# Two routed layers on one core: the selector matmuls give way to an addition on GpSimd and to rows below the tables

## The chip, the cores and the metric

One core of one Trainium2 chip. The time is the device time of one launch in microseconds, median of several runs.

## The reference, cut to what matters

`x` is 128 sequences of 64 tokens of 256 features. Every sequence `b` has an expert `e0 = itok_B_0_7[b]` (of 8) and a domain `d = itok_B_0_15[b]` (of 16).

```
h = gelu(x @ Wi[e0] + bi[e0]);  o = h @ Wo[e0] + bo[e0]          # 256 -> 1024 -> 256
r = layernorm(o + x);           x1 = r * gamma[e0] + beta[e0]
a = gelu(x1 @ down_W.T + down_b)                                 # 256 -> 64
e = a @ expert_W[d].T + expert_b[d] + domain_emb[d]
out = layernorm(e @ up_W.T + up_b + x1) * ln_gamma + ln_beta
```

## The kernel before

Two sequences make a tile of 128 tokens; a sort on the chip puts sequences of one expert together, so that 60 tiles have one expert and the last four ("mixed") may have one for each half. The loop over tiles is a pipeline of 64 + 5 steps, written out by hand for each engine: in step `i` TensorE does the first product of tile `i`, the second of `i-1`, the transposes of `i-2`, the down product of `i-3` and the up product of `i-4`. Steps 6 to 53 run in a hardware loop of 8 steps a round, the others are unrolled. Engines wait for each other by counting semaphores; SyncE issues nearly all DMAs on one queue.

Every value that goes through TensorE is split into an f16 high part and an f16 low part, and a product is three matmuls (high x high, low x high, high x low), L1138 to L1140 and L1149 to L1151. Weights of an expert come in chunks of 128x512 (`stage`); ScalarE makes the high part (L619), VectorE the low one (L867). In the same way `x_T` (x with the features on the partitions) gives `x_hi` (L664) and `x_lo` (L863), gelu's result `h` (L695) gives `h_hi` (L706) and `h_lo` (L896), in two halves a tile.

The first residual `r` (L912) is taken from the PSUM bank `p_o` and `x_nat`, its statistics by L915 and L927, the power -1/2 of the variance on GpSimd (L584), the normal form `z` on VectorE (L950). TensorE turns it into `p_t` (L1187), ScalarE and VectorE scale it by gamma into `yT_hi` (L743) and `yT_lo` (L980), and the down product (L1162 to L1164) makes `p_d`. Gelu of it is `a` (L720), which is put into `a1s` as high part on all partitions (L725) and then as low part on the lower 64 (L938). `up` multiplies `a1s` with two tables of each sequence's domain (`ctab`, high and low part; expert_W and up_W are multiplied into one beforehand, entry by entry, in `rounds`), L1179, four matmuls. The second norm goes L922, L932, L943, power L588 on GpSimd, `y` L958; GpSimd multiplies by ln_gamma and adds ln_beta (L560, L562), and multiplies `z` by gamma for the second residual (L579, `yg`).

What depends on the expert or domain only as one row of 256 is added by a matmul with a selector: `sel_tile` (128x128, a 1 or a scale at the rows of this tile's sequences; copied by GpSimd from `sel`, L603) times `bo_parts` into `p_o` (L1256), the output bias, and times `parts` into `p_u` (L1175), everything that is added in the up product. Both have three f16 parts of each row. They are made at the start on GpSimd by `split_rows` (L524 to L528), `parts` in its step 1.

```
mm(p_u[:, 0:D], sel_tile[:, four, :], parts[:, :], start=True, stop=False)
...
mm(p_o[:, 0:D], sel_tile[:, (four + 3) % 4, :], bo_parts[:, :], start=True, stop=False)
```

## Time and profile before

| | before |
|---|---|
| median of 3 runs | 472.51 us (472.42 to 473.59) |
| the profiled execution's own time | 472.13 us |
| its span in the trace | 470.4 us |
| TensorE, VectorE, ScalarE, GpSimd busy | 448.5, 379.4, 350.8, 339.4 us |
| granted clock, mean | 0.988 |
| DMA moved | 44.38 MB, 94 GB/s |

PE is TensorE's matmuls, PEld its weight loads, DVE VectorE, ACT ScalarE, POOL GpSimd, SP SyncE; SPq and ACTq are their DMA issues. A row of the timeline has start and duration in us, engine, line, operation, output and inputs, and in square brackets how long the engine sat idle before it and whom it waited for. The start of a matmul's row is when it enters the array; its duration includes the pipeline, so the cost of a matmul is the distance to the next one.

### The profile page before, as it was taken

The page shows a single profiled execution, that of the slowest core. Times are in us where ns is not written, and L with a number is a line of the kernel's source. Part 1 is how long each engine was busy: PE and PEld are TensorE (multiplying, and loading weights), DVE is VectorE, ACT ScalarE, POOL GpSimd, SP SyncE. Part 2 cuts the span into 40 slices and gives each one's busy share as a digit, 9 for nine tenths or more (in the row PEclk, how much of TensorE's full clock was granted, in tenths as well). Part 3 has the DMA queues.
Part 4 walks back from the last instruction along what each step waited for, and adds up shares of the span by engine and source line. Part 5 has one row for each costly group of instructions (what it writes and reads, how often), then busy time and mean ns, then how long its engine had stood idle before and what let it go on. Part 6 is the DMA issues. An engine that isn't in the chain of part 4 may idle for free.

```text
span 470.4 us, 19196 instructions
## 1 busy us (share of the span) xinstructions
PE 448.5 (95%) x5856; PEld 414.9 (88%) x5857; DVE 379.4 (81%) x1052; ACT 350.8 (75%) x1094; POOL 339.4 (72%) x559
## 2 busy tenths in 40 slices
PE   3898999999999999999999999999999999999973
PEld 2687999999999999999999999999999999998961
DVE  7769888888888888888888888888888887776465
ACT  2689877787777877778777787777877767776721
POOL 5244777877778877897778977888788887764533
PEclk9999999999999999999999999999999999999995
DMA  4852244433433333334333343334432222221101
GB/s 104 289 166 80 68 107 122 113 93 102 106 104 103 92 104 106 106 97 110 92 102 99 103 106 90 104 96 106 106 92 81 57 63 66 64 58 36 26 24 33
DMA packets 66810, 44.38 MB, mean 94 GB/s; under 512 B 41537, under 2 KB 58322, under 8 KB 66642
## 3 DMA queue, kind: packets, MB, share of 16 engines
q1 hardware_dynamic: 65744, 43.68, 34.7%
q8 instruction: 21, 0.34, 0.3%
q10 hardware_dynamic: 1026, 0.21, 0.2%
q14 instruction: 19, 0.16, 0.1%
HBM read 35.47 MB, written 8.39 MB: 93 GB/s over the span
## 4 chain that ended last, share of the span: by engine, by line
PE 88%; DVE 4%; issue 2%; ACT 2%; POOL 1%; DMA 1%; POOLq 0%; ACTq 0%; DVEq 0%
PE p_o L1150 12%; PE p_o L1149 12%; PE p_o L1151 12%; PE p_h L1138 12%; PE p_h L1139 12%; PE p_h L1140 12%; PE p_u L1179 6%; PE p_t L1187 3%; PE p_u L1175 2%; PE p_d L1162 2%; PE p_o L1256 1%; PE p_d L1164 1%; PE p_d L1163 1%; ACT W L619 1%; DMA x_T<-in_xT 1%
## 5 line engine op out<-in xcount | busy, mean ns | idle before, releaser
L1138 PE MATMUL p_h<-x_hi,W 128*128 128x128 f16 (+1 forms) x1088 | 184.5, 217 | 1.0 <-DVE x_lo L863 0.5
L1139 PE MATMUL p_h<-x_lo,W 128*128 128x128 f16 (+1 forms) x1088 | 184.4, 217 | 0.0
L1140 PE MATMUL p_h<-x_hi,W 128*128 128x128 f16 (+1 forms) x1088 | 184.3, 217 | 0.0
L695 ACT ACTIVATE h<-p_h,bi_tile 128x128 f32<-128x128 f32 (+1 forms) x544 | 148.6, 358 | 0.0
L1151 PE MATMUL p_o<-W,h_lo 128*128 x512 | 139.6, 273 | 0.0
L1150 PE MATMUL p_o<-W,h_hi 128*128 x512 | 139.6, 273 | 0.0
L1149 PE MATMUL p_o<-W,h_hi 128*128 x512 | 139.6, 273 | 0.0
L1138 PEld LDWEIGHTS p_h<-x_hi,W 128*128 x1088 | 105.9, 98 | 5.4 <-issue 2.8
L1139 PEld LDWEIGHTS p_h<-x_lo,W 128*128 x1088 | 106.0, 98 | 1.3
L1140 PEld LDWEIGHTS p_h<-x_hi,W 128*128 x1088 | 106.0, 98 | 0.0
L588 POOL TENSOR_TENSOR rs<-mv,neg_half 128x1 f32<-128x1 f32 x64 | 55.5, 866 | 60.0 <-DVE mv L943 60.0
L720 ACT ACTIVATE a<-p_d,gb_tile 128x128 f32<-128x128 f32 (+1 forms) x68 | 24.1, 360 | 87.2 <-PE p_d L1164 87.2
L896 DVE SCALAR_TENSOR_TENSOR h_lo<-h,h_hi 128x512 f16<-128x512 f32 (+1 forms) x128 | 83.9, 658 | 1.6 <-ACT h_hi L706 1.6
L706 ACT ACTIVATE h_hi<-h 128x512 f16<-128x512 f32 (+1 forms) x128 | 79.1, 621 | 2.0
L603 POOL COPY sel_tile<-sel 128x128 f16 (+1 forms) x64 | 77.7, 1213 | 0.6 <-issue 0.6
L938 DVE SCALAR_TENSOR_TENSOR a1s<-a,a1s 64x128 f16<-64x128 f32 x64 | 18.5, 290 | 49.5 <-ACT a1s L725 49.3
L560 POOL TENSOR_TENSOR y<-y,lng 128x256 f32<-128x256 f32 x60 | 43.6, 726 | 19.2 <-DVE h_lo L896 17.0
L1150 PEld LDWEIGHTS p_o<-W,h_hi 128*128 128x128 f16 x512 | 50.1, 98 | 5.8
L1151 PEld LDWEIGHTS p_o<-W,h_lo 128*128 128x128 f16 x512 | 50.1, 98 | 5.8
L1149 PEld LDWEIGHTS p_o<-W,h_hi 128*128 128x128 f16 x512 | 50.1, 98 | 4.4
L584 POOL TENSOR_TENSOR rs<-mv,neg_half 128x1 f32<-128x1 f32 x64 | 35.4, 553 | 24.3 <-DVE mv L927 24.3
L980 DVE SCALAR_TENSOR_TENSOR yT_lo<-p_t,gb_tile,yT_hi 128x128 f16<-128x128 f32 (+1 forms) x136 | 39.5, 333 | 12.2 <-ACT yT_hi L743 12.2
(179 smaller groups left out, 899.8 us busy)
## 6 DMA issues: line engine op xcount, KB each, us to landing
stage<-in_w SPq DMA_DIRECT2D x56, 256.0 KB, 2.7
x_nat<-in_x SPq DMA_DIRECT2D x128, 64.0 KB, 2.1
out<-y SPq DMA_DIRECT2D x128, 64.0 KB, 2.0
x_T<-in_xT SPq DMA_DIRECT2D x126, 64.0 KB, 2.2
W<-in_w SPq DMA_DIRECT2D x8, 256.0 KB, 3.6
g_t<-in_gamma SPq DMA_DIRECT2D x1, 1024.0 KB, 8.0
W<-in_expert_W SPq DMA_DIRECT2D x2, 128.0 KB, 3.0
upT<-in_up_W SPq DMA_DIRECT2D x2, 64.0 KB, 2.6
```

The costliest lines, as they stand in the source:

```text
L560: pool.tensor_tensor(last, last, lng[:, :], ALU.mult).then_inc(zg_done, 1)
L588: pool.tensor_tensor(rs[:, 1:2], mv[:, 1, 1:2], neg_half[:, 0:1], ALU.pow).then_inc(rs2_done, 1)
L603: pool.tensor_copy(sel_tile[:, four, :].rearrange("p (n s) -> p n s", n=2), sel[:, bass.ds(2 * i, 2)].unsqueeze(2).to_broadcast([P, 2, S]))\
L695: ins = nc.scalar.activation(h[:, c, mine], p_h[parity][:, c, mine], ACT.Gelu, bias=bi_tile[:, parity, n, c:c + 1], scale=1.0 / (XS * WS))
L706: ins = nc.scalar.activation(out, h[:, cols_h, mine], ACT.Copy, scale=HS)
L896: ins = v.scalar_tensor_tensor(lo[at], h[:, cols_h, mine], HS, hi[at], ALU.mult, ALU.subtract)
L1138: mm(out, hi, x_hi[:, parity, k, mine], start=(k == 0), stop=False)
L1139: mm(out, hi, x_lo[:, parity, k, mine], start=False, stop=False)
L1140: ins = mm(out, lo, x_hi[:, parity, k, mine], start=False, stop=(k == KD - 1))
L1149: mm(p_o[:, 0:D], h_high[at], hi, start=False, stop=False)
L1150: mm(p_o[:, 0:D], h_high[at], lo, start=False, stop=False)
L1151: ins = mm(p_o[:, 0:D], h_low[at], hi, start=False, stop=(j == KI - 1 and n == len(places) - 1))
```

## The change

1. The output bias is added on GpSimd: `bo_t` holds `bo` of all experts on all partitions (one more broadcast load of 1,024 KB, issued ahead of `g_t`), and in step `i` GpSimd adds tile `i-1`'s row to `x_nat` between the two powers. The first residual waits for that (`xb_done`) and not for the load.
2. What is added in the up product lies in `ctab` itself. The low part of the table has only 64 rows; rows 64 to 90 of it now hold the added rows in three f16 parts (3 of the entry itself, 24 of the experts). `parts` goes out to a DRAM tensor after step 1 of SyncE and comes back into these rows with four DMAs in step 2. A second block `a1o` (91 rows used) has the high part of `a` above and constants below: ScalarE writes it after `yT_hi`, with a scale and a bias for each partition (`keeps`, and a fourth column of `gb_tile`). `up` is `a1s` x high, `a1o` x low and added rows, for each of the two sequences.
3. `sel`, `sel_tile`, its copy on GpSimd, both selector matmuls and what made them at the start (on VectorE, TensorE, GpSimd and ScalarE) are gone.
4. `x_T`, `x_hi`, `x_lo` are laid out as (sequence, feature half, 64 tokens): a load of a sequence is 512 B a partition in one piece, and the moving operand of the first product has two runs of 64 columns.
5. SyncE reads the record of two steps at once; VectorE does `y` (`normal_2`) behind the weight chunk and not ahead of it.

```diff
+        bo_t = sb("bo_t", [P, E0 * D])
-        x_hi = sb("x_hi", [P, 2, KD, P], f16)
+        x_hi = sb("x_hi", [P, 2, 2, KD, S], f16)
...
@@ SyncE
+            sp.dma_start(bo_t[:, :], t["bo"].partition_broadcast(P)).then_inc(bo_in, 16)
             sp.dma_start(g_t[:, :], t["gamma"].partition_broadcast(P)).then_inc(g_in, 16)
...
+                    if parity == 0:
+                        two = 12 if exists(i + 1 + 2) or exists(i + 1 - 5) else 6
+                        record[:] = indices(sp, 6 * i + IDX_SP, two, B - 1)
...
+                if isinstance(i, int) and i == 1:
+                    sp.wait_ge(parts_ready, 1)
+                    sp.dma_start(added[:, :], parts[0:PARTS * GROUP, :]).then_inc(added_out, 16)
+                if isinstance(i, int) and i == 2:
+                    sp.wait_ge(added_out, 16)
+                    by_part = added[:, :].rearrange("(q g) c -> q g c", g=GROUP)
+                    sp.dma_start(ctab[OWN_ROWS, :, 1, :], by_part[:, 0:ENTRIES, :]).then_inc(added_in, 16)
+                    for q in range(PARTS):
+                        sp.dma_start(ctab[A + PARTS + E0 * q:A + PARTS + E0 * (q + 1), :, 1, :],
+                                     by_part[q, ENTRIES:ENTRIES + E0, :].unsqueeze(1)
+                                     .to_broadcast([E0, ENTRIES, D])).then_inc(added_in, 16)
@@ GpSimd
-            pool.wait_ge(b_ready, 1)
-            split_rows(b_s[:, :], b_rest, b_16, bo_parts)
...
                     pool.tensor_tensor(rs[:, 0:1], mv[:, 0, 1:2], neg_half[:, 0:1], ALU.pow).then_inc(rs1_done, 1)
+                if exists(i - 1):
+                    pool.wait_ge(xnat_in[1 - parity], loads(i - 1, 1 - parity, 2))
+                    if isinstance(i, int) and i == 1:
+                        pool.wait_ge(bo_in, 16)
...
+                        pool.tensor_tensor(x_nat[:, 1 - parity, :], x_nat[:, 1 - parity, :],
+                                           bo_t[:, bass.ds(e_last * D, D)], ALU.add).then_inc(xb_done, 1)
...
-                    need(pool, a1_done, i - 3)
+                    need(pool, a1o_done, i - 3)
...
-                    pool.tensor_copy(sel_tile[:, four, :].rearrange("p (n s) -> p n s", n=2),
-                                     sel[:, bass.ds(2 * i, 2)].unsqueeze(2).to_broadcast([P, 2, S]))\
-                        .then_inc(sel_done, 1)
@@ ScalarE, behind yT_hi
+                if exists(i - 3):
+                    for n in range(2 if mixed(i - 3) else 1):
+                        mine = slice(n, n + 1) if mixed(i - 3) else slice(0, 2)
+                        ins = nc.scalar.activation(own(a1o[:, :, :])[:, mine, :],
+                                                   a1[:, :].rearrange("p (n s) -> p n s", n=2)[:, mine, :],
+                                                   ACT.Identity, scale=keeps[:, :],
+                                                   bias=gb_tile[:, 1 - parity, n, KD + 1:GB])
+                    ins.then_inc(a1o_done, 1)
@@ VectorE
-                    dve.wait_ge(xnat_in[parity], loads(i - 2, parity, 2))
+                    dve.wait_ge(xb_done, i - 1)
...
-                if exists(i - 4):
-                    normal_2()
                 for j, (m, place_n, slot_n) in chunks(i, weights):
                     dve.wait_ge(w_hi, j + 1)
                     low(m, place_n, stage[:, slot_n, :]).then_inc(w_lo, 1)
+                if exists(i - 4):
+                    normal_2()
@@ TensorE
-                    pe.wait_ge(sel_done, i - 3)
-                    mm(p_u[:, 0:D], sel_tile[:, four, :], parts[:, :], start=True, stop=False)
                     pe.wait_ge(a1_lo, i - 3)
+                    pe.wait_ge(a1o_done, i - 3)
                     for n in range(2):
-                        for part in range(2):
-                            ins = mm(p_u[:, 0:D], a1s[:, n, :], up_weights(n, part), start=False,
-                                     stop=(n == 1 and part == 1))
+                        mm(p_u[:, 0:D], a1s[:, n, :], up_weights(n, 0), start=(n == 0), stop=False)
+                        ins = mm(p_u[:, 0:D], a1o[LOW_ROWS, n, :], up_weights(n, 1), start=False, stop=(n == 1))
...
-                    pe.wait_ge(sel_done, i)
-                    mm(p_o[:, 0:D], sel_tile[:, (four + 3) % 4, :], bo_parts[:, :], start=True, stop=False)
```

GpSimd's queue in one step of the hardware loop, before: the two products of the output (`y`), `yg`, the two powers, then the copies for gamma and for the selector.

```order
L560 TENSOR_TENSOR y<-y,lng 128x256 [waits hlo_half]
L562 TENSOR_TENSOR y<-y,lnb 128x256 [waits zg_done]
L579 ISA [waits z1_done]
L579 TENSOR_TENSOR yg<-z,g_t 128x256
L584 TENSOR_TENSOR rs<-mv,neg_half 128x1 [waits mv1_done]
L588 TENSOR_TENSOR rs<-mv,neg_half 128x1 [waits mv2_done]
L596 ISA [waits a1_done]
L596 COPY gb_tile<-gb_c 128x3
```

The same step in the changed kernel:

```order
L590 TENSOR_TENSOR y<-y,lng 128x256 [waits hlo_half]
L592 TENSOR_TENSOR y<-y,lnb 128x256 [waits zg_done]
L609 ISA [waits z1_done]
L609 TENSOR_TENSOR yg<-z,g_t 128x256
L614 TENSOR_TENSOR rs<-mv,neg_half 128x1 [waits mv1_done]
L618 ISA
L630 ISA [waits xnat_in0]
L630 TENSOR_TENSOR x_nat<-x_nat,bo_t 128x256
L635 TENSOR_TENSOR rs<-mv,neg_half 128x1 [waits mv2_done]
L643 ISA [waits a1o_done]
L643 COPY gb_tile<-gb_c 128x4
```

The addition stands between the two powers, and gamma's copy waits for `a1o`.

TensorE's up product in the hardware loop, before:

```order
L1175 MATMUL p_u<-parts,sel_tile 128x256 [waits sel_done,r2_done]
L1179 MATMUL p_u<-ctab,a1s 128x256 [waits a1_lo]
L1179 MATMUL p_u<-ctab,a1s 128x256 x3
```

and in the changed kernel:

```order
L1207 MATMUL p_u<-ctab,a1s 128x256 [waits a1o_done,a1_lo,r2_done]
L1208 MATMUL p_u<-ctab,a1o 128x256
L1207 MATMUL p_u<-ctab,a1s 128x256
L1208 MATMUL p_u<-ctab,a1o 128x256
```

One matmul is gone, and the whole group waits for `a1o` ahead of its first.

## Rows read from the trace of the kernel before

**Rows 1.** Window (length; PE, PEld, DVE, ACT, POOL busy; clock, DMA); chain by engine.

```profile
110.00:360.00 250.00, 249.96 (x3288) 235.57 (x3287) 210.56 (x574) 200.14 (x615) 201.02 (x307) 1.00 0.38 101
...
PE 88%; DVE 4%; issue 2%; ACT 2%; POOL 1%; DMA 1%; POOLq 0%; ACTq 0%; DVEq 0%
```

**Rows 2.** Chain in order (start, us, what); timeline of one step (start, us, engine, line, operation).

```profile
236.41 0.44 PE p_u L1179 x4
...
242.92 0.44 PE p_u L1179 x4
...
242.65 0.27 PE L1175 MATMUL p_u<-parts,sel_tile 128*128 128x256 f16 x1
...
245.88 0.27 PE L1256 MATMUL p_o<-bo_parts,sel_tile 128*128 128x256 f16 x1
```

**Rows 3.** ScalarE in the same step, and the group of `a1s` by line.

```profile
241.72 0.64 ACT L706 ACTIVATE h_hi<-h 128x512 f16<-128x512 f32 x1
...
244.40 0.37 ACT L720 ACTIVATE a<-p_d,gb_tile 128x128 f32<-128x128 f32 x1 [1.23 <-PE p_d L1164]
...
L725 ACT ACTIVATE a1s<-a 128x128 f16<-128x128 f32 x64 | 19.9, 311 | 2.0
```

**Rows 4.** The same step on VectorE, then GpSimd, then TensorE's transposes.

```profile
239.70 0.41 DVE L950 TENSOR_SCALAR z<-r,mv,rs 128x256 f32<-128x256 f32 x1
...
241.29 0.68 DVE L896 SCALAR_TENSOR_TENSOR h_lo<-h,h_hi 128x512 f16<-128x512 f32 x1
...
245.21 0.29 DVE L938 SCALAR_TENSOR_TENSOR a1s<-a,a1s 64x128 f16<-64x128 f32 x1 [0.79 <-ACT a1s L725]
...
245.65 0.65 DVE L896 SCALAR_TENSOR_TENSOR h_lo<-h,h_hi 128x512 f16<-128x512 f32 x1
...
242.21 0.72 POOL L560 TENSOR_TENSOR y<-y,lng 128x256 f32<-128x256 f32 x1
...
244.39 0.55 POOL L584 TENSOR_TENSOR rs<-mv,neg_half 128x1 f32<-128x1 f32 x1
245.81 0.89 POOL L588 TENSOR_TENSOR rs<-mv,neg_half 128x1 f32<-128x1 f32 x1 [0.88 <-DVE mv L943]
...
240.79 0.38 PE L1187 MATMUL p_t<-ident,z 128*128 128x128 f32 x2
```

**Rows 5.** Timeline at 43 us: GpSimd and VectorE at once.

```profile
43.11 0.73 POOL L579 TENSOR_TENSOR yg<-z,g_t 128x256 f32<-128x256 f32 x1
...
43.18 1.22 DVE L867 SCALAR_TENSOR_TENSOR W<-stage,W 128x512 f16<-128x512 f32 x1
```

**Rows 6.** Timeline of TensorE in a mixed tile: columns of 128, then of 64.

```profile
431.00 0.22 PE L1162 MATMUL p_d<-yT_hi,down_hi 128*128 128x128 f16 x1
...
431.17 0.19 PE L1138 MATMUL p_h<-x_hi,W 128*128 128x64 f16 x1
...
431.52 0.20 PE L1138 MATMUL p_h<-x_hi,W 128*128 128x64 f16 x1
```

**Rows 7.** Start: SyncE's issue, ScalarE's wait, and the window with its DMA share.

```profile
18.91 0.42 SPq L429 DMA_DIRECT2D g_t<-in_gamma  x1
...
28.03 0.42 ACT L664 ACTIVATE x_hi<-x_T 128x256 f16<-128x256 f32 x1 [1.32 <-DMA x_T<-in_xT]
...
22.00:26.00 4.00, 4.00 (x60) 3.52 (x58) 2.62 (x6) 3.97 (x12) 0.54 (x3) 1.00 1.02 370
```

**Rows 8.** Start: GpSimd's first split and first power, TensorE's first down.

```profile
25.52 0.40 POOL L524 CAST W<-W 128x256 f16<-128x256 f32 x1
...
35.05 0.90 POOL L584 TENSOR_TENSOR rs<-mv,neg_half 128x1 f32<-128x1 f32 x1 [4.58 <-DVE mv L927]
...
40.30 0.23 PE L1162 MATMUL p_d<-yT_hi,down_hi 128*128 128x128 f16 x1 [1.03 <-DVE yT_lo L980]
```

**Rows 9.** Drain: ScalarE's last `yT_hi` and TensorE's up group.

```profile
459.84 0.93 ACT L743 ACTIVATE yT_hi<-p_t,gb_tile 128x64 f16<-128x64 f32 x4 [1.75 <-POOL gb_tile L596]
...
460.47 0.37 PE L1175 MATMUL p_u<-parts,sel_tile 128*128 128x256 f16 x1 [0.74 <-issue]
```

More of the change, by code:

```diff
@@ L88, in build @@
         ident = sb("ident", [P, P])
-        sel = sb("sel", [P, SLOTS], f16)
-        parts = sb("parts", [P, D], f16)
-        bo_parts = sb("bo_parts", [P, D], f16)
+        keeps = sb("keeps", [P, 1])
         x_nat = sb("x_nat", [P, 2, D])
-        x_T = sb("x_T", [P, 2, KD, P])
-        x_hi = sb("x_hi", [P, 2, KD, P], f16)
-        x_lo = sb("x_lo", [P, 2, KD, P], f16)
+        x_T = sb("x_T", [P, 2, 2, KD, S])
+        x_hi = sb("x_hi", [P, 2, 2, KD, S], f16)
+        x_lo = sb("x_lo", [P, 2, 2, KD, S], f16)
         r1 = sb("r1", [P, D])
@@ L114, in build @@
         a1s = sb("a1s", [P, 2, P], f16)
-        a1_own = a1s[:, :, :].rearrange("p n t -> p (n t)")
+        a1o = sb("a1o", [P, 2, P], f16)
         st2 = sb("st2", [P, 9])
@@ L506, in _ @@
             link(pool.memset(embb[HALF[0], :, :], 0.0))
-            link(pool.memset(parts[:, :], 0.0))
-            link(pool.memset(bo_parts[:, :], 0.0))
+            link(pool.memset(keeps[:, :], 0.0))
+            link(pool.memset(keeps[HALF[0], :], AS))
+            takes = gb_c[:, :, KD + 1]
+            link(pool.memset(takes, 0.0))
+            link(pool.memset(gb_c[OWN_ROWS, :, KD + 1], AS * CS))
+            for q in range(PARTS):
+                link(pool.affine_select(out=takes, in_=takes, compare_op=ALU.not_equal, fill=AS * CS,
+                                        base=-(A + PARTS + E0 * q), pattern=[[-1, E0]], channel_multiplier=1))
             pool.wait_ge(emb_in, 2 * 16)
@@ L663, in high_x @@
                 need(act, s1_half, 2 * i - 2)
-                nc.scalar.activation(x_hi[:, parity, :, :], x_T[:, parity, :, :], ACT.Copy, scale=XS)\
+                nc.scalar.activation(flat(x_hi, parity), flat(x_T, parity), ACT.Copy, scale=XS)\
                     .then_inc(xhi_done, 1)
@@ L724, in step @@
                     need(act, up_done, i - 3)
-                    nc.scalar.activation(own(P), a1[:, :].rearrange("p (n s) -> p n s", n=2), ACT.Copy, scale=AS)\
+                    nc.scalar.activation(own(a1s[:, :, :]), a1[:, :].rearrange("p (n s) -> p n s", n=2), ACT.Copy, scale=AS)\
                         .then_inc(a1_hi, 1)
@@ L1137, in first_product @@
                         out = p_h[parity][:, c, mine]
-                        mm(out, hi, x_hi[:, parity, k, mine], start=(k == 0), stop=False)
-                        mm(out, hi, x_lo[:, parity, k, mine], start=False, stop=False)
-                        ins = mm(out, lo, x_hi[:, parity, k, mine], start=False, stop=(k == KD - 1))
+                        x_high, x_low = [x[:, parity, n:n + 1, k, :] if mixed(i) else x[:, parity, :, k, :]
+                                         for x in (x_hi, x_lo)]
+                        mm(out, hi, x_high, start=(k == 0), stop=False)
+                        mm(out, hi, x_low, start=False, stop=False)
+                        ins = mm(out, lo, x_high, start=False, stop=(k == KD - 1))
                 return ins
```

117 lines of the change are left out of this document (53 added, 64 removed).

## The prediction

> **What bounds the kernel now.** I read the windows first, since a mean over the span mixes stages. From 110 to 360 us TensorE is busy 249.96 of 250 us, VectorE 210.56, ScalarE 200.14, GpSimd 201.02 [rows 1], and the chain of waits that ended last is 88% TensorE [rows 1]. The chain's rows for the four up matmuls stand 6.51 us apart [rows 2]: the step of one tile is TensorE's own queue, full, at the full clock (1.00 in the window). A matmul taken out of it is worth its pitch, as long as nobody else needs more than the shorter step. So three questions remain: what the others have in hand in a step, and what the change does to start and drain, where TensorE does wait.
>
> **Selector matmuls, -13.5 us.** A step loses the `sel_tile` x `parts` matmul at the head of `up` (at 242.65) and the `sel_tile` x `bo_parts` one at the head of the second product (at 245.88) [rows 2]. Four matmuls of the same 256 columns take 0.44 us in the chain [rows 2], 0.11 each; the duration 0.27 in a row is pipelined and is not the price. The up itself keeps four. 64 tiles give 128 matmuls; two before 40 us and three in the drain stand where TensorE waits anyway, so 123 x 0.11 = 13.5 us. The step becomes 6.51 - 0.22 = 6.29 us.
>
> **ScalarE's block, 0.** `a1o` is one more 128x128 activation, as `a1s`, 0.31 us [rows 3]. ScalarE idles 1.23 us a step before `a` [rows 3]; 1.23 - 0.22 - 0.31 leaves 0.70. Its place is between `yT_hi` and `h_hi`, so it starts where `h_hi` does now, 241.72, and ends at 242.03; TensorE comes to `up` at 242.65 [rows 2, 3], now 0.11 earlier. Margin 0.5 us. Behind it are `h_hi`, `x_hi` and the next weight chunk, each 0.31 later; what VectorE makes of that `h_hi` starts only at 245.65 [rows 4]. Were the idle time gone, the cost would be 0.1 us a step or more.
>
> **GpSimd and VectorE, +1.0 us.** GpSimd loses the copy of the selector and gains `x_nat + bo`, a 128x256 tensor_tensor like `y * lng`, 0.72 us [rows 4]. It isn't the length that matters but the place. Now GpSimd starts `y` once VectorE's `h_lo` is through (241.29 + 0.68 = 241.97) and works to the end of the first power at 244.39 + 0.55 = 244.94, 2.73 us after its start, in the stretch in which VectorE reads PSUM or takes statistics. Then it pauses 0.88 us [rows 4], and the new addition falls into that pause: about 244.7 to 245.5. VectorE wants `a1s` at 245.21, an instruction with two SBUF inputs. What such a meeting costs shows at 43 us: GpSimd's `yg` ran from 43.11 to 43.84, and VectorE's `W`, sent at 43.18, took 1.22 us, where `h_lo` of the same 128x512 takes 0.68 [rows 4, 5]: it stood until 0.12 us before GpSimd's end. As a loop: from `a1s` to the end of the next `h_lo` VectorE needs 241.97 + 6.51 - 245.21 = 3.27 us without a gap; from there to the end of GpSimd's addition are 2.73 + 0.72 = 3.45. If `a1s` waits it out each time, the loop is 3.27 + 3.45 - 0.12 = 6.60 us. If `a1s` comes ahead of the addition, the next `h_lo`, 0.44 us behind it, waits in its place, and the loop is 6.60 - 0.44 = 6.16. A step of 6.29 lies between them, so I expect the two to alternate with VectorE up to 0.45 us late. That is bearable: `z` ends at 240.11 and TensorE turns it at 240.79 [rows 4], 0.68 ahead, 0.57 after the change. I charge 0.02 us for each of some 47 full steps, 1.0 us; the ends are 0 and 47 x 0.31 = 14.6 us. Moving `y` behind the weight chunk gives the second power, now behind the addition, 0.6 us more time, and costs nothing.
>
> **Moving operand in two runs, 0.** `x_hi` and `x_lo` are now two runs of 64 columns in a 128-column matmul. No row has this form. The last tiles show 64-column matmuls, twelve in 431.52 - 431.17 = 0.35 us, 0.029 each, and 128-column ones, three in 0.17, 0.056 each [rows 6]. As two separate matmuls each would cost 0.058: 48 a step make at most 0.1 us, some 6 us in all. The low end is 0, and I take it, since the columns are the same in number; a gain is excluded.
>
> **Start, +3.0 us.** SyncE puts `bo` for all experts (1,024 KB, as `g_t`) ahead of `g_t` at 18.9 us. The queue is full then: 1.02 of the DMA engines' time and 370 GB/s from 22 to 26 us, and ScalarE waited 1.32 us for `x_T` of tile 2, which stood behind `g_t` [rows 7]. 1.05 MB more at 370 GB/s is 2.8 us. ScalarE takes this wait ahead of tile 1's gelu, tables and `h_hi`, so all of it moves by 2.8, and so do VectorE's first residual and `z`, and the `yT_lo` for which TensorE waited 1.03 us at 40.30 [rows 8]. GpSimd is delayed as well: it now waits for `x_nat` of tile 0 (in the queue behind `x_T`, so not before 30.8), adds, and only then splits the rows, 25.52 to 35.05 - 4.58 = 30.47 now, until some 36.6; it has 4.58 us to spare before the power at 35.05 [rows 8], which will be wanted at 37.9. It has to read its indices first, so I add 0.2. Ends: 0, if the shorter list of packets for `x_T` (512 B and not 256 B) and the earlier tile rows pay it back, and 5, if GpSimd is late by 2 us more. SyncE's new wait for `parts_ready`, to some 36.6, holds back `x_T` of tile 4, two natural tiles and a chunk; none is wanted before the first down, at 40.30 now and 43.3 then. The transfers of the added rows go out in step 2 and are read by `up` of step 4, a step of 6.5 us behind that down: 0. Two steps' records in one load save SyncE some register loads; nobody waits for those.
>
> **Drain, +1.0 us.** There ScalarE's order is `yT_hi` of the last tile, then `a1o` of the one before, in two halves. `yT_hi` runs from 459.84 to 460.77, and TensorE began the up group at 460.47 [rows 9]; now that must wait for `a1o`, at about 461.2: later by 0.4 net. The last up waits for one more block behind `a1s`, 0.2. At step 64 `h_hi` is 0.4 later and the first residual with it, for which TensorE stood ready.
>
> **The sum**, against the profiled execution's own 472.1 us (span 470.4): 472.1 - 13.5 + 1.0 + 3.0 + 1.0 = 463.6. The median of the runs lies 0.4 higher, at 472.5, so 464.0 us, or 1.8% less. Measurement can tell about 0.3% (1.4 us) from no change.
>
> **The rivals.**
> - *The start does not get longer* (chance 0.15). For: TensorE at 30.9 us does not itself wait for tile 2 now, and packets of `x_T` are halved. Against: ScalarE's visible wait. 464.0 - 3.0 = 461.0, and 460 if VectorE's lateness is free too.
> - *GpSimd's addition sets the step: slower* (0.11). If `a1s` loses the race each time, the loop of 6.60 us is longer than the 6.51 of before, whatever TensorE saved. For: the addition starts 2.73 us after `h_lo`, and VectorE would be there after 6.29 - 3.27 = 3.02, so at first it does lose. Against: once it is late, it meets the addition in the other order. It decides from the point where VectorE can't be 0.3 us late without TensorE waiting for `z`. Price 47 x 0.31 = 14.6 instead of 1.0: 477.6 us. The Trainium skill, SBUF — State Buffer, "Who interferes with whom", has the rule: a VectorE instruction with two SBUF inputs and a GpSimd one that reads SBUF exclude each other, and the second to issue waits for the whole of the first. The meeting at 43 us agrees, up to the last 0.12 us.
> - *In between* (0.14): half of the steps lose, or two runs cost 0.1 us a step: 468 to 472.
> - *It doesn't do what it says* (0.02): TensorE finds a new wait at `up` on `a1o` each step; 472 or a little more.
> The forecast itself has 0.58, with 461.5 to 468.
>
> Faster by over 0.3% than 472.5 are the forecast, the first rival and nearly all between: 0.85; within 0.3% 0.04; slower 0.11. The range, with the lower rival in and the slow one out, is 459.0 to 471.0.
>
> **What would show it.** Right: up groups 6.29 us apart in the chain, TensorE still full from 110 to 360, `a1s` or the `h_lo` behind it lengthened by 0.2 to 0.5 us under GpSimd's addition; ScalarE's idle time before `a` near 0.7 us; its wait for `x_T` of tile 2 near 4 us, and TensorE at its first down at about 43.3. Wrong: up groups at 6.5 us or more, TensorE idle before the transposes on `z` (then it is the port) or before `up` (then `a1o`); 128-column matmuls on `x_hi` over 0.056 apart.

## The result, and the profile after

| | before | changed |
|---|---|---|
| median | 472.47 us (471.86 to 473.59, 4 runs) | 468.88 us (468.71 to 469.13, 4 runs) |
| span of the profiled execution | 470.4 us | 467.0 us |
| TensorE, VectorE, ScalarE, GpSimd busy | 448.5, 379.4, 350.8, 339.4 us | 435.8, 392.2, 378.4, 343.1 us |
| first up product | 46.77 | 50.28 us |
| from there to the up of tile 54 | 352.44 | 344.52 us |
| from there to the end | 71.19 | 72.20 us |

The ratio is 0.9923, with a 95% interval of 0.9909 to 0.9937: 3.6 us faster, where 8.5 were forecast. The last three rows of the table cut the span into start, 54 steps, and end, by the times at which an up group begins. The sum of the three changes is +3.5 - 7.9 + 1.0 = -3.4 us. The forecast was near for the start (+3.0); the steady part should have given 10.9, and the end should have got 0.65 shorter, where it got 1.0 longer.

The window of 250 us of the changed kernel (columns as in [rows 1]) and its matmuls at a round of the hardware loop, which begins every eighth step:

```profile
110.00:360.00 250.00, 248.59 (x3296) 231.89 (x3294) 223.47 (x588) 221.11 (x668) 205.08 (x314) 1.00 0.36 102
```

```profile
210.00 0.27 PE L1207 MATMUL p_u<-ctab,a1s 128*128 x1
...
216.42 0.23 PE L1168 MATMUL p_h<-x_hi,W 128*128 128x128 f16 x1 [0.29 <-issue]
...
216.91 0.27 PE L1207 MATMUL p_u<-ctab,a1s 128*128 x1
```

TensorE was busy all the time before [rows 1]; now 1.4 us are missing from the window. VectorE has 12.9 us more to do in it, though the change gave it nothing new there. The ordinary step is 6.30 us, as forecast (6.29). The step in which the loop turns round is 6.91 (210.00 to 216.91); before it was 6.71 (209.90 to 216.61), so it did not lose 0.22 but gained 0.20. The first matmul of the new round starts 6.42 us after the up group, where in an ordinary step it starts at 5.96.

An ordinary step on VectorE and GpSimd, the one that answers to [rows 4], and ScalarE's to [rows 3]:

```profile
241.26 0.68 DVE L933 SCALAR_TENSOR_TENSOR h_lo<-h,h_hi 128x512 f16<-128x512 f32 x1
...
244.64 0.29 DVE L974 SCALAR_TENSOR_TENSOR a1s<-a,a1s 64x128 f16<-64x128 f32 x1 [0.47 <-ACT a1s L759]
245.07 0.99 DVE L933 SCALAR_TENSOR_TENSOR h_lo<-h,h_hi 128x512 f16<-128x512 f32 x1
245.99 0.40 DVE L986 TENSOR_SCALAR z<-r,mv,rs 128x256 f32<-128x256 f32 x1
...
242.02 0.73 POOL L590 TENSOR_TENSOR y<-y,lng 128x256 f32<-128x256 f32 x1 [0.95 <-DVE h_lo L933]
...
244.71 0.81 POOL L630 TENSOR_TENSOR x_nat<-x_nat,bo_t 128x256 f32<-128x256 f32 x1
...
241.36 0.52 ACT L785 ACTIVATE a1o<-a,gb_tile,keeps 128x128 f16<-128x128 f32 x1
243.82 0.37 ACT L754 ACTIVATE a<-p_d,gb_tile 128x128 f32<-128x128 f32 x1 [0.60 <-PE p_d L1194]
```

GpSimd's addition (244.71 to 245.52) starts while `a1s` runs and is over 0.45 us after `h_lo` was sent; that `h_lo` takes 0.99 instead of 0.65, so it stood about 0.34, until 0.1 us before the addition's end. `z` ends at 246.39, 4.21 us after the up group of its step (242.18), not 3.97, and VectorE's `h_lo` of the first half 5.40 after it and not 5.15. This is the second of the two forecast orders (`a1s` first, `h_lo` held up). The forecast had the two alternate; here it is the second in nearly all steps. `a1o` takes 0.52 us, not 0.31. It ends 6.02 us after the up group, and TensorE's next up stands at 6.30.

The start, to be held against [rows 7, 8], and TensorE's waits in the last steps, of which before there were none for ScalarE's block:

```profile
29.99 0.42 ACT L698 ACTIVATE x_hi<-x_T 128x256 f16<-128x256 f32 x1 [4.58 <-DMA x_T<-in_xT]
...
30.56 0.88 POOL L630 TENSOR_TENSOR x_nat<-x_nat,bo_t 128x256 f32<-128x256 f32 x1 [15.34 <-DMA x_nat<-in_x]
...
38.42 0.56 POOL L614 TENSOR_TENSOR rs<-mv,neg_half 128x1 f32<-128x1 f32 x1 [1.81 <-issue]
...
415.65 0.27 PE L1207 MATMUL p_u<-ctab,a1s 128*128 x1 [0.90 <-ACT a1o L785]
...
452.06 0.27 PE L1207 MATMUL p_u<-ctab,a1s 128*128 x1 [1.76 <-ACT a1o L785]
...
457.10 0.37 PE L1207 MATMUL p_u<-ctab,a1s 128*128 x1 [2.08 <-ACT a1o L785]
...
460.45 0.37 PE L1207 MATMUL p_u<-ctab,a1s 128*128 x1 [1.70 <-ACT a1o L785]
```

### The profile page after: what moved, and what is told of

The parts are those of the page before. It is cut to its first block, busy times and chain, and to the rows that moved or that the text cites. A ratio compares the mean times of both kernels' runs of the same rounds, so it can differ in the third digit from the quotient of the medians.

```text
span 467.0 us, 19001 instructions
## 1 busy us (share of the span) xinstructions
PE 435.8 (93%) x5724; PEld 399.7 (86%) x5725; DVE 392.2 (84%) x1049; ACT 378.4 (81%) x1161; POOL 343.1 (73%) x560
## 4 chain that ended last, share of the span: by engine, by line
PE 84%; DVE 3%; issue 3%; ACT 3%; SPq 2%; DMA 2%; POOL 2%; POOLq 1%; ACTq 0%; DVEq 0%
PE p_h L1168 12%; PE p_o L1179 12%; PE p_o L1180 12%; PE p_o L1181 12%; PE p_h L1170 11%; PE p_h L1169 11%; PE p_u L1207 3%; PE p_u L1208 3%; PE p_t L1215 3%; DMA x_nat<-in_x 2%; PE p_d L1192 2%; PE p_d L1194 1%; PE p_d L1193 1%; ACT h L729 1%; ACT yT_hi L777 1%
## 5 line engine op out<-in xcount | busy, mean ns | idle before, releaser
L933 DVE SCALAR_TENSOR_TENSOR h_lo<-h,h_hi 128x512 f16<-128x512 f32 (+1 forms) x128 | 97.9, 767 | 1.9 <-ACT h_hi L740 1.9
L740 ACT ACTIVATE h_hi<-h 128x512 f16<-128x512 f32 (+1 forms) x128 | 80.1, 629 | 2.0
L635 POOL TENSOR_TENSOR rs<-mv,neg_half 128x1 f32<-128x1 f32 x64 | 58.9, 920 | 13.4 <-DVE mv L979 13.1
L630 POOL TENSOR_TENSOR x_nat<-x_nat,bo_t 128x256 f32<-128x256 f32 x60 | 46.6, 776 | 15.3 <-DMA x_nat<-in_x 15.3
L974 DVE SCALAR_TENSOR_TENSOR a1s<-a,a1s 64x128 f16<-64x128 f32 x64 | 22.1, 346 | 34.6 <-ACT a1s L759 34.4
L614 POOL TENSOR_TENSOR rs<-mv,neg_half 128x1 f32<-128x1 f32 x64 | 35.2, 550 | 18.0 <-DVE mv L962 16.1
L777 ACT ACTIVATE yT_hi<-p_t,gb_tile 128x128 f16<-128x128 f32 (+1 forms) x136 | 42.2, 380 | 7.5 <-PE p_t L1215 5.6
```

The source lines that it names most:

```text
L630: pool.tensor_tensor(x_nat[:, 1 - parity, :], x_nat[:, 1 - parity, :], bo_t[:, bass.ds(e_last * D, D)], ALU.add).then_inc(xb_done, 1)
L635: pool.tensor_tensor(rs[:, 1:2], mv[:, 1, 1:2], neg_half[:, 0:1], ALU.pow).then_inc(rs2_done, 1)
L740: ins = nc.scalar.activation(out, h[:, cols_h, mine], ACT.Copy, scale=HS)
L777: ins = nc.scalar.activation(yT_hi[:, k, mine], turned_z[:, mine], ACT.Copy, scale=gb_tile[:, parity, n, k:k + 1])
L933: ins = v.scalar_tensor_tensor(lo[at], h[:, cols_h, mine], HS, hi[at], ALU.mult, ALU.subtract)
```

## The experiments

All are edits of the changed kernel, except where it is said. Start, 54 steps and end are cut as above, in us of the profiled execution; turn is the mean step at a round of the loop (the step in which the loop goes back to its first instruction), without the first one at step 6.

| run | median us (range) | start | 54 steps | end | turn |
|---|---|---|---|---|---|
| before | 472.47 (471.86 to 473.59) | 46.77 | 352.44 | 71.19 | 6.70 |
| changed | 468.88 (468.71 to 469.13) | 50.28 | 344.52 | 72.20 | 6.90 |
| changed, once more | 469.20 (468.72 to 470.47) | 51.42 | 344.35 | 72.23 | 6.90 |
| no addition | 464.38 (463.82 to 465.50) | 48.65 | 341.61 | 72.34 | 6.58 |
| addition first | 467.30 (466.40 to 467.72) | 51.07 | 342.47 | 72.36 | 6.58 |
| addition first, in the loop | 466.92 (466.53 to 467.86) | 50.68 | 342.25 | 72.27 | 6.58 |
| before, plus an addition | 476.23 (475.00 to 476.71) | 47.43 | 355.92 | 71.15 | 7.11 |
| tables loaded later | 465.91 (465.51 to 466.46) | 47.22 | 344.79 | 72.29 | 6.90 |
| rows split later | 475.33 (474.93 to 476.05) | 55.77 | 346.33 | 72.20 | 6.89 |
| rows split later, and the loads | 471.38 (470.37 to 472.17) | 50.19 | 346.20 | 72.21 | 6.90 |
| rows split later, the loads, addition first | 468.55 (467.65 to 470.29) | 51.62 | 344.58 | 72.30 | 6.58 |
| loads later, split first | 464.70 (464.31 to 465.20) | 45.40 | 344.93 | 72.17 | 6.90 |
| `a1o` early at the end | 468.77 (467.95 to 469.26) | 50.01 | 344.46 | 71.73 | 6.89 |
| `a1o` early in the drain | 469.57 (469.03 to 469.89) | 50.28 | 345.80 | 71.22 | 6.89 |
| one block | 470.41 (468.18 to 471.14) | 50.43 | 345.44 | 71.73 | 6.89 |
| loop and drain | 465.61 (465.43 to 466.18) | 50.20 | 342.23 | 71.37 | 6.57 |
| `a1o` early in the loop too | 465.98 (465.65 to 466.27) | 50.56 | 342.25 | 71.49 | 6.57 |
| `z` first | 481.91 (481.14 to 482.79) | 50.89 | 357.24 | 72.57 | 7.04 |
| all mended | 460.39 (460.00 to 460.97) | 44.39 | 342.45 | 71.36 | 6.57 |
| all mended, `z` first | 468.75 (468.30 to 469.07) | 45.05 | 350.39 | 71.16 | 6.89 |

The start of one and the same kernel varies: in the nine kernels whose code for it is that of the changed one it is 50.01 to 51.42 us. A difference of a microsecond there shows nothing.

My theory after the result: GpSimd's addition meets VectorE's two-input instructions, and this costs TensorE time where the loop turns; the start is the queue; the end is `a1o`. Rivals: TensorE's own program at the turn, `a1o` there, a start bound by GpSimd, an end bound by the last tiles' chain.

### The addition and the steady part

```diff
-                    pool.tensor_tensor(x_nat[...], x_nat[...], bo_t[...], ALU.add).then_inc(xb_done, 1)
...
-                    dve.wait_ge(xb_done, i - 1)
+                    dve.wait_ge(xnat_in[parity], loads(i - 2, parity, 2))
```

> Leaves out part of the computation: the addition of the experts' output bias to x_nat on GpSimd (its table is still loaded), so the output lacks that bias; VectorE's first residual waits for x_nat's load instead. Theory A (GpSimd's addition and VectorE meet; VectorE's lateness of some 0.3 us is what is exposed where the hardware loop turns round): the second half's h_lo is back at 0.65 us (0.99 in the changed kernel), z ends 0.25 us earlier in the step, ordinary steps stay at 6.30, and the six steps at a turn of the loop fall from 6.9 to about 6.5 (6.7 before, less 0.22 for the two matmuls): 2.5 us, and 0.5 us more from the steps just behind them. GpSimd's row splits end 0.8 us earlier in the start: up to 0.8 more. Together 465.0 us. Theory B (the turn of the loop costs more for another reason, TensorE's own program or ScalarE's new block): turns stay at 6.9, and only the start's share comes, 468.1 us.

464.38 us; turns 6.58, ordinary steps 6.30, and the second step behind a turn 6.30 instead of 6.35 to 6.39. The steady part gives 2.9 us, the start 1.6. Theory A.

```diff
@@ GpSimd, step: the block "x_nat + bo" moved
+                if exists(i - 1): ... x_nat + bo
                 if exists(i - 2):
                     ... first power
-                if exists(i - 1): ... x_nat + bo
```

> GpSimd's addition goes ahead of the first power, right behind yg, into the stretch in which VectorE reads PSUM or takes statistics. Theory A (the meeting with VectorE is what costs): h_lo of the second half back at 0.65 to 0.7 us, turns of the loop from 6.9 to about 6.6, time 466.5 us. Theory B (GpSimd is late then): the first power, 0.7 us later, holds back z by the same or more, TensorE waits for z before the transposes, steps of 6.5 us or more, 475 us or more.

467.30 us. The same work in another place gives 2.1 of these 2.9 us back in the steady part, and the start is 0.8 longer, which is within its variation; TensorE waits 2.23 us there for `z` of tile 0, 1.82 in the changed kernel. Since that clouds the run, the same edit from step 6 on alone, beside the changed kernel once more:

> The changed kernel with GpSimd's addition ahead of the first power from step 6 on alone; the first steps stay as they are. With the addition ahead from the first step on, the start was 0.8 us longer (z of tile 0 waited 2.23 us) and the rest 2.4 us shorter. Theory A (meeting): start 50.3, ordinary steps 6.30, turns 6.6: 466.5 us, with a small spread. Theory B (something of the gain came from the first steps' order): 467.3 us or more.

> The changed kernel once more, unaltered, as the measure for the runs beside it. Two runs that differ from it only in the drain came out at 469.6 and 470.4 us, though their drains were shorter in the trace, with single steps of 6.4 to 6.6 us in the middle. Theory A (where GpSimd's addition meets VectorE, the length of the steps itself varies from execution to execution and from chip to chip): 468.5 to 470.5 us here, with a spread of over 1 us, and single ordinary steps over 6.40 us in the profile. Theory B (those two edits did it): 468.9 us with 0.4 us of spread, ordinary steps as before.

466.92 against 469.20 us, and 2.1 us in the 54 steps. Against the addition first from the start on (467.30) the difference is within the spread. The changed kernel's own spread is 1.75 us here, as its theory A expects. The ordinary steps of over 6.40 us that it expects too did not show in this profile. VectorE and GpSimd with the addition ahead of the power, the same stretch as above:

```profile
243.66 0.29 DVE L994 SCALAR_TENSOR_TENSOR a1s<-a,a1s 64x128 f16<-64x128 f32 x1 [0.79 <-ACT a1s L779]
244.09 0.65 DVE L953 SCALAR_TENSOR_TENSOR h_lo<-h,h_hi 128x512 f16<-128x512 f32 x1
244.65 0.41 DVE L1006 TENSOR_SCALAR z<-r,mv,rs 128x256 f32<-128x256 f32 x1
```
```profile
242.89 0.73 POOL L629 TENSOR_TENSOR x_nat<-x_nat,bo_t 128x256 f32<-128x256 f32 x1
243.57 0.55 POOL L634 TENSOR_TENSOR rs<-mv,neg_half 128x1 f32<-128x1 f32 x1
```

The addition is over at 243.62, before `a1s` is sent; `h_lo` is back at 0.65, `z` ends 3.87 us after the up group. The power, which starts 2.38 us after the up group and not 2.02, still comes in time.

Then the same load on the kernel before:

```diff
@@ kernel before, GpSimd, behind the first power
+                if not isinstance(i, int) or 6 <= i < TILES:
+                    pool.tensor_tensor(spare[:, parity, :], lng[:, :], lnb[:, :], ALU.add)
```

> The kernel before, with one 128x256 addition from and into spare buffers put on GpSimd in each step from the 6th, behind the first power, where the change has its own; nobody waits for it. Theory A (meeting of GpSimd and VectorE, exposed at the turns of the loop): ordinary steps stay at 6.51, h_lo of the second half grows from 0.65 to about 0.9 us, turns of the loop go from 6.70 to some 6.9 us: 474 us. Theory B (the turns' length comes of something else in the change): nothing changes, 472.5 us. Should VectorE lose every race, every step grows: 480 us or more.

476.23 us, 3.8 more than before, where theory A had 474; 3.5 us of it are in the 54 steps. Turns 7.11; ordinary steps 6.51 and 6.64 in turn. Two steps of VectorE:

```profile
241.05 0.85 DVE L941 SCALAR_TENSOR_TENSOR a1s<-a,a1s 64x128 f16<-64x128 f32 x1 [0.57 <-ACT a1s L728]
242.04 0.65 DVE L899 SCALAR_TENSOR_TENSOR h_lo<-h,h_hi 128x512 f16<-128x512 f32 x1
...
247.68 0.29 DVE L941 SCALAR_TENSOR_TENSOR a1s<-a,a1s 64x128 f16<-64x128 f32 x1 [0.57 <-ACT a1s L728]
248.11 0.99 DVE L899 SCALAR_TENSOR_TENSOR h_lo<-h,h_hi 128x512 f16<-128x512 f32 x1
```

Here the two orders do alternate: `a1s` held up by 0.56 us, then `h_lo` by 0.34. An addition whose result nobody waits for made the 54 steps 3.5 us longer. What it holds up in the trace is VectorE; TensorE's program is that of before.

### What makes the turn longer

`z` was the nearest suspect: TensorE turns it 0.23 us after its end in the changed kernel, 0.57 with the addition first, 0.68 before.

```diff
@@ VectorE, steps 6 to 63
+                    normal_1()
                     split_h(i - 1, 1 - parity, 1)
-                    normal_1()
```

> The changed kernel with one thing moved on VectorE, from step 6 to the last full step: z, which TensorE transposes, goes ahead of h_lo's second half; GpSimd's order stays as the change has it. z has one input from SBUF, so it can run under GpSimd's addition, and it ends at about 3.3 us after the up group instead of 4.21, where TensorE starts the transposes at 4.44. h_lo's second half then runs from 3.3 us on, mostly behind the addition. Theory A (a turn of the loop is long because z is finished only 0.23 us before TensorE wants it): turns of 6.6 us or less, steps behind a turn 6.30: 466.5 us. Theory B (the length of GpSimd's addition or the number of meetings matters by itself, wherever z stands): turns stay at 6.9, 468.9 us. If h_lo's second half, which TensorE wants at 4.8 us, becomes the late one, ordinary steps grow over 6.30 us.

> As e12_all_mended, and z ahead of h_lo's second half as in e17_z_first. There z already had 0.57 us to spare and a turn of the loop took 6.58 us. Theory A (the excess at a turn goes on falling with z's lead): turns of 6.5 us, 459.9 us. Theory B (the rest of the excess, 0.28 us, is TensorE's own program at the turn): turns stay at 6.58 and the time at 460.4.

Both theories fell. 481.91 us, 13 us slower than the changed kernel; and 468.75, 8.4 slower than without the edit. `z` ends 3.75 and 3.61 us after the up group, earlier than in any other kernel, and a turn is still 0.4 us longer than an ordinary step. The ordinary step itself is 6.63 and 6.48 us. VectorE, GpSimd and TensorE in the first of the two:

```profile
132.81 0.78 DVE L974 SCALAR_TENSOR_TENSOR a1s<-a,a1s 64x128 f16<-64x128 f32 x1 [0.63 <-ACT a1s L759]
133.74 0.37 DVE L986 TENSOR_SCALAR z<-r,mv,rs 128x256 f32<-128x256 f32 x1
134.03 0.68 DVE L933 SCALAR_TENSOR_TENSOR h_lo<-h,h_hi 128x512 f16<-128x512 f32 x1
```
```profile
132.71 0.74 POOL L630 TENSOR_TENSOR x_nat<-x_nat,bo_t 128x256 f32<-128x256 f32 x1
```
```profile
136.99 0.27 PE L1210 MATMUL p_u<-ctab,a1s 128*128 x1 [0.18 <-ACT a1o L785]
```

Now the addition is sent 0.1 us ahead of `a1s`, in each ordinary step, and `a1s` waits it out. `h_lo` of the second half starts 3.67 us after the up group instead of 2.90. ScalarE's next gelu may only overwrite `h` when this `h_lo` has read it; behind that gelu stand `yT_hi` and `a1o`, which starts at 5.97 instead of 5.50, and TensorE's up waits for it. In the second kernel the addition is earlier and ends 0.1 us into `a1s`, which takes its 0.29 us, and the step is 6.48 all the same: `h_lo` behind `z` ends at 4.21, `a1o` at 6.34, the up follows 0.14 later. So of the 0.33 us that a step grows, the order alone is 0.18 and the held up `a1s` 0.15. `h_lo` has some slack (it ends at 3.89 in the changed kernel, and the step is 6.30), but less than `z`'s new place takes.

A turn is longer than an ordinary step by 0.19 us before, 0.28 with the addition first or absent, 0.60 in the changed kernel and before with an addition, and 0.4 in the two with `z` first, where the next two steps, 6.30 and 6.57 or 6.30 and 6.30, win it back. That the last kernel has it without a held up `a1s` or `h_lo` tells against the meeting as such, and `z`'s early end tells against `z`. Its rows at a turn (VectorE, GpSimd and TensorE; up at 207.83), and the one that answers in the changed kernel (up at 210.00, first matmul of the new round at 216.42):

```profile
210.29 0.29 DVE L1002 SCALAR_TENSOR_TENSOR a1s<-a,a1s 64x128 f16<-64x128 f32 x1 [0.63 <-ACT a1s L793]
211.95 0.42 DVE L927 SCALAR_TENSOR_TENSOR x_lo<-x_T,x_hi 128x256 f16<-128x256 f32 x1
...
209.68 0.73 POOL L631 TENSOR_TENSOR x_nat<-x_nat,bo_t 128x256 f32<-128x256 f32 x1
...
214.23 0.23 PE L1199 MATMUL p_h<-x_hi,W 128*128 128x128 f16 x1 [0.28 <-issue]
```
```profile
214.13 0.41 DVE L899 SCALAR_TENSOR_TENSOR x_lo<-x_T,x_hi 128x256 f16<-128x256 f32 x1
```

What the two share is the lateness of VectorE behind `z` and `h_lo`. The operand that TensorE waits for at the head of a step is `x_lo`, VectorE's next instruction. It ends, on the mean of the turns, 4.55 us after the up group in the changed kernel, 4.54 in "all mended, `z` first", 4.69 with `z` first and 4.87 before with an addition, and the new round's first matmul starts at 6.41, 6.41, 6.53 and 6.72: 1.84 to 1.87 us behind it each time. With the addition first it is 4.20 and 6.10 (1.89), before 4.30 and 6.32 (2.02). In an ordinary step 1.41 us are enough (4.55 and 5.96). No run moved `x_lo` alone, and VectorE's instructions behind it move with it; so this is a reading, and which wait it is stays open.

One more suspect, `a1o`, could be tested by its place:

```diff
@@ ScalarE: a1o right behind a1s from step 6 to 59 and in the drain, on top of "addition first, in the loop"
```

> As e13_add_first_in_loop, with a1o right behind a1s on ScalarE from step 6 to 59 and in the drain. Of a turn of the loop 0.1 us is still unexplained (6.58 us, where 6.70 less 0.22 is 6.48), and TensorE shows a gap of 0.13 us before the up there. Theory A (that gap is a1o's): turns of 6.5 us, 0.6 us less in all. Theory B (it is TensorE's own program at the turn): turns stay at 6.58. In both the gelu of each tile's first half starts 0.5 us later; if the second product comes to wait for h_lo, steps are longer than 6.30 us, and the time is over 467 us.

465.98 us, about the drain's gain alone (below); turns stay at 6.57. Theory B: `a1o` has no part in the turn, and with the addition first its place in the loop costs nothing.

### The start

```diff
@@ SyncE
-            ... bo_t, g_t, lng, lnb behind the first weight chunks
+                if isinstance(i, int) and i == 0:
+                    ... bo_t, g_t, lng, lnb behind load_natural(0), that is behind x_T of tile 2
```

> The loads of bo_t, g_t and the layer norm's two vectors are issued by SyncE behind x_T of tile 2 and x_nat of tile 0 instead of ahead of them. Theory A (the start's 3.5 us are the queue: 1 MB more ahead of x_T of tile 2): ScalarE's wait of 4.58 us for x_T of tile 2 goes, TensorE's first down comes at some 40 instead of 43.65, and the up of step 4 at 47 or a little before instead of 50.28: 465.5 us. Theory B (TensorE's own work and GpSimd's row splits bound the start as soon as the transfer is early): the wait goes, but z of tile 0 still waits for GpSimd, whose addition now waits for bo_t, and the gain is 1 us or less: 468 us.

465.91 us, the first up at 47.22: Theory A, 3.1 of the 3.5 us (2.8 against the shortest of the nine starts). TensorE still waits 1.04 us for `z` of tile 0.

```diff
@@ GpSimd, SyncE: split_rows from the end of step 1 to the end of step 2, its DMAs from steps 1, 2 to 2, 3
@@ second run, SyncE, too: bo_t in step 0 behind x_nat of tile 0, g_t, lng, lnb in step 1 behind x_nat of tile 1
```

> The changed kernel with only GpSimd's splitting of the added rows moved, from the end of step 1 to the end of step 2. Theory A (of the start's 3.5 us some 1.3 are GpSimd, whose first power stood behind the splits: VectorE's variance was there at 37.1, the power ran at 38.42): TensorE's wait of 1.82 us for z of tile 0 falls to about 0.5, the up of step 4 comes 1.3 us earlier: 467.6 us. Theory B (the wait for x_T of tile 2 is all of it): no change, 468.9 us.

> The changed kernel with its start rearranged in two ways: bo_t is loaded behind x_nat of tile 0, and gamma and the layer norm's vectors behind x_nat of tile 1; GpSimd splits the added rows at the end of step 2 instead of step 1, so that the first power does not stand behind them (SyncE's transfers of the added rows move by one step too). Theory A (the start's loss is the queue and GpSimd's lateness together): with the loads alone TensorE still waited 1.04 us for z of tile 0, which waited for GpSimd, and ScalarE 1.61 us for x_T of tile 3; both go, and the up of step 4 comes at 46.0 to 46.3 us (50.28 in the changed kernel, 47.22 with the loads alone): 464.7 us. Theory B (the start is bound by TensorE's own work once the loads are later, or the added rows now come too late for the up of step 4): no better than 465.9 us.

475.33 and 471.38 us, where 467.6 and 464.7 were hoped for: the first is 6.5 slower than the changed kernel. The power of tile 0 came earlier, and with both edits the first down too (37.73 us), but the added rows came too late for the first up:

```profile
55.77 0.40 PE L1207 MATMUL p_u<-ctab,a1s 128*128 x1 [5.07 <-DMA ctab<-added]
```
```profile
48.00:56.00 8.00, 2.31 (x22) 1.92 (x23) 5.10 (x10) 2.87 (x7) 2.08 (x4) 0.89 0.44 109
56.00:60.00 4.00, 4.00 (x36) 3.82 (x35) 1.28 (x5) 1.20 (x5) 1.24 (x2) 0.50 0.03 8
```

The price of 0 for the transfers of the added rows was right for the change as it is, but with some 3 us to spare: here SyncE had issued the last of them at 51.5 us and the up went on 4.3 us later; in the changed kernel that was 42.8 and the up came at 50.28. And TensorE, idle for 5.07 us before, was granted half its clock (0.50, 1.2 GHz) from 56 to 60 us; the step behind the wait took 8.81 us instead of 6.30. The splits belong earlier, not later:

```diff
@@ GpSimd
-                if isinstance(i, int) and i == 1:
+                if isinstance(i, int) and i == 0:
                     pool.wait_ge(u_ready, 1)
...
@@ SyncE: the loads as in the second run above
```

> The loads as in e5_start_mended (bo_t behind x_nat of tile 0, gamma and the layer norm's vectors behind x_nat of tile 1), but GpSimd splits the added rows at the end of step 0, when it stood idle for 7 us and more, and not after the addition; SyncE's transfers of the added rows stay in steps 1 and 2. Theory A (the splits have to be done both before the first power and in time for the up of step 4, which waited 4.8 us for the added rows when they came a step later): the first down comes at some 38 us as in e5_start_mended, the up of step 4 at 44.5, nobody waits for the added rows: 463.0 us. Theory B (the splits, from 18.5 us on, now collide with VectorE's splits of the weight chunks, or SyncE's wait for them holds up loads): up of step 4 at 47 us, 466 us.

464.70 us, first up at 45.40, 4.9 us earlier than in the changed kernel and 1.4 earlier than before: between the two theories (463.0 and 466). There the up of tile 1 waits 0.62 us for `a1o` (a step of 7.08).

### The end

```diff
@@ ScalarE, from step 60 on
                     ... a1s
+                    ... a1o
                 ... gelu, h_hi, yT_hi
-                    ... a1o
```

> From step 60 on ScalarE writes a1o right behind a1s, not behind yT_hi. Theory A (TensorE's four waits for a1o, 0.90, 1.76, 2.08 and 1.70 us, are due to its place): those waits go or shrink to some 0.6 us of a1o behind a1s; from the up at 394.8 to the end 72.2 us become about 69.5: 466.3 us. Theory B (in these steps ScalarE or the chain tile by tile is the bound, and a1o is only what it comes last by): gelu and h_hi of the mixed tiles, now behind a1o, are 0.5 to 0.8 us later, and the time stays within 0.7 us of 468.9.

468.77 us: Theory B in the main. The step of 7.81 us falls to 6.73, the next grows from 9.66 to 10.41; the end gives 0.5 us, which the median doesn't show.

```diff
@@ ScalarE: the same from step 64 on alone
@@ TensorE, in the drain: a1s x table for both sequences, then the wait for a1o, then a1o x table
```

> Only in the drain (from step 64) ScalarE writes a1o right behind a1s, and TensorE's up there takes its two a1s matmuls first and waits for a1o only ahead of the other two. Theory A (moving it for the mixed tiles too was what gave the gain back, 10.40 us for a step of 9.66): the ups' waits of 1.76 and 2.08 us shrink by some 0.8 in all, the last of 1.70 us by 0.3; 468.9 less 1.1 is 467.8 us. Theory B (the chain of the last tile, z to yT_lo to down, bounds the drain whatever a1o does): 468.6 us or more.

> As e13_add_first_in_loop, and the drain as in e8_drain_block (a1o right behind a1s from step 64 on, TensorE's wait for it behind the two a1s matmuls). Theory A (a1o's place costs 1.0 us in the drain, 72.2 to 71.2 us from the up of tile 54 in the trace, which the variation of the steps hid): 1.0 us less than e13_add_first_in_loop. Theory B (the drain's 1.0 us is not real, or given back): the same as e13_add_first_in_loop within 0.4 us.

The first came out at 469.57 us, no better than the changed kernel (468.88 and 469.20), though its end is 1.0 us shorter: in the middle, where nothing was edited, three steps took 6.44, 6.64 and 6.50 us, and others up to 6.55. There GpSimd's copy was held up too, and VectorE after it:

```profile
125.37 0.94 POOL L643 COPY gb_tile<-gb_c 128x4 f32 x1
126.25 0.98 POOL L575 COPY bi_tile<-bi_c 128x8 f32 x1
```
```profile
130.01 0.83 DVE L980 SCALAR_TENSOR_TENSOR a1s<-a,a1s 64x128 f16<-64x128 f32 x1 [0.59 <-ACT a1s L771]
```

(0.34, 0.66 and 0.29 us elsewhere.) On top of the addition first, where the engines don't meet, the same drain gives 1.3 us, 465.61 against 466.92, and the end 0.9: Theory A. With the meeting in it, the middle varies with nothing edited there (344.35 to 345.80 us in the table), and that hid the gain; with the addition first it is 342.23 to 342.47 in five kernels.

```diff
@@ ScalarE
-                    for n in range(2 if mixed(i - 3) else 1):
-                        mine = slice(n, n + 1) if mixed(i - 3) else slice(0, 2)
+                    for n in range(1):
+                        mine = slice(0, 2)
```

> Leaves out part of the computation: for the tiles of two experts a1o is written in one instruction with the first expert's column, so the second half of those tiles gets the wrong expert's row. Theory A (the tail's extra microsecond is ScalarE, which has 0.8 us more a mixed tile where I reckoned with 0.4): 0.3 us less for each of the four mixed tiles where ScalarE is late, and in the drain: 468.9 less 1.0 is 467.9 us. Theory B (in the mixed steps TensorE's own queue is the bound): only the last up's wait is shorter, 468.6 us.

470.41 us, with runs from 468.18 to 471.14, where 467.9 or 468.6 was expected. In this kernel the second half of a mixed tile gets the first half's row. By the median it is a miss for both theories; by the trace the end is 0.5 us shorter. Inconclusive for the time.

### All together

```diff
@@ "addition first" from step 4, on top of the start with the split in step 2
```

> The start rearranged as in the run before this one, and from step 4 on GpSimd's addition ahead of its first power. Both theories of the parts hold apart, so the gains should add: the up of step 4 at some 46.1 us, ordinary steps 6.30, turns of the loop 6.6 instead of 6.9: 464.7 less 2.1 is 462.6 us. If the two share a cause (GpSimd has no time left over), less: 464 us.

468.55 us for the 462.6 expected, because the start was not mended (first up 51.62, for the same reason as above); its 54 steps, less the one behind that wait (9.20 us), gain 2.8 us. Then with the start of the split in step 0, the addition first from step 6, and the drain:

> All together: the loads and the splitting as in e10_split_first, the addition ahead of the first power in the hardware loop and behind it (not in the first steps), the drain as in e8_drain_block. If the causes are separate the gains add: 463.0 for the start, 2.2 less for the turns of the loop, 1.1 less in the drain: 459.7 us. If the start gives less, 461 to 463 us.

460.39 us, where 459.7 were expected if the gains add; ratio 0.9752 to before (0.9739 to 0.9764): 8.5 us better than the changed kernel and 11.7 better than before (472.10, measured beside it).

```profile
110.00:360.00 250.00, 250.00 (x3324) 235.57 (x3322) 213.78 (x592) 221.77 (x673) 218.03 (x317) 1.00 0.37 101
```

TensorE is full again from 110 to 360 us. VectorE is busy for 213.78 us, 9.7 less than in the changed kernel, with the same instructions and a step of the same 6.30 us.

## Why the prediction was right or wrong

The direction and the range held (468.9 in 459.0 to 471.0), the gain was less than half. Step by step, in the trace (3.4 us where 8.5 were reckoned):

- **Selector matmuls, -13.5.** Right in the ordinary step, which went from 6.51 to 6.30 us for 6.29.
- **GpSimd and VectorE, +1.0: this step failed.** The meeting was seen, its place and VectorE's lateness (0.24 us at `z`, within the 0.45 given) were right, and ordinary steps show none of it, as forecast. That the two orders would alternate was wrong here: it was `h_lo` nearly each time. What failed is "bearable: `z` ends 0.68 ahead of TensorE", and so 0.02 us for each full step: I priced a lateness by the ordinary steps alone and never looked at the turn of the loop, though the steps of 6.7 us stood in the trace of before. The 54 steps should have lost 108 matmuls, 11.9 us, and lost 7.9: the term measured +4.0. Of these 2.9 go with the addition (344.52 to 341.61), 2.3 of them with its place in the loop alone (342.25), 0.6 at the first turn (6.95, without the addition 6.33). The rest, 1.1, comes without any meeting too: 0.1 at each of the five later turns, 0.01 at each other step. And `z` was the wrong witness: with `z` early a turn stays as long. By which wait VectorE's lateness reaches TensorE there is open; the traces point at `x_lo` or what follows it.
- **ScalarE's block, 0.** The price was wrong, 0.52 us and not 0.31 (idle before `a` 0.60, not 0.70), the conclusion right for the loop: moving it there, with the addition first, changed nothing. The margin was not 0.5 us, though. `a1o` ends 0.28 before the next up, and where it came later (with `z` first) the up followed 0.14 behind its end, so 0.14 was left. The row that I took does not fit: `a1s` has constants for scale and bias, `a1o` takes both from memory. The Trainium skill, ScalarE: Activation LUTs, "What ACT_TABLE_LOAD costs", gives 93 ns more for each operand that is one value a partition. By that an estimate for two is 0.19, and the trace shows 0.21. In two halves it is 0.78 in all.
- **Two-run operand, 0.** Right: 48 such matmuls are in the ordinary step, which is 6.30 us long.
- **Start, +3.0.** Right, 3.5, and 4.7 in the second profile of the same kernel. ScalarE's wait came out at 4.58 (about 4 forecast), TensorE's first down at 43.65 us (43.3). With the loads later 3.1 us are gone. GpSimd's splits ended at 36.61 (36.6), but its power, at 38.42 (37.9), held `z` up by 1.5; I had that in the step, but not that VectorE was ready at 36.9. The added rows for the first up, which I had at 0, were in time.
- **Drain, +1.0.** Too small. From the up of tile 54 to the end 15 matmuls should have gone, 1.65 us, so the term measured 1.0 + 1.65 = 2.7. The place of `a1o` in the drain is 0.9 to 1.0 of it, which is the forecast term. What the forecast lacked is the other 1.7: the first mixed tile's step, where the up waits 0.90 us for `a1o` behind the longer gelus, and ScalarE's 0.78 us for each mixed tile. That these two make it up is not shown. Moving `a1o` there gave only 0.5 back, so which share is ScalarE's stays open.
- **The rivals.** "GpSimd's addition sets the step" did not happen in the changed kernel, but with one instruction moved `a1s` does lose the race in each ordinary step. The step is then 6.63 us for the 6.60 that I had worked out, 481.9 us for 477.6. That it comes so near is partly luck: the moved instruction alone makes it 6.48. The Trainium skill, SBUF — State Buffer, "Who interferes with whom", says that the second to issue waits for the whole of the first: `a1s`, sent 0.1 us behind an addition of 0.74, took 0.49 us more, so it stood until about 0.15 us before the addition's end.

## What to carry to other kernels

Work given to GpSimd is not free because GpSimd is idle: place it where VectorE reads PSUM or takes statistics, not where it has two inputs in SBUF, and look at how much longer VectorE's instructions become. A saving a step has to be followed through the steps that are not ordinary: the turn of a loop, the first and last of an unrolled stretch, tiles in two halves; here most of the 4.0 of 11.9 us that the steady part lost went at them. A table that nobody needs before the third tile should stand in the queue behind the inputs of the first ones.
